# A six-layer linear-attention block with a quantised feed-forward: query and key products in three fp16 parts, softmax kept in PSUM, one merged root, a new instruction order

## What is computed

```python
mod = (_silu(c) @ wmod).reshape(8, 6, 1, -1)                     # sa, ca, ga, sb, cb, gb
ga = (2 * (ga >= 0) - 1) * jnp.maximum(jnp.abs(ga), 0.25)       # gb alike
h = _layernorm(x) * (1 + ca) + sa
for i in range(6):                                               # _L0_attn_ref
    xn = _layernorm(x, ln1_w[i], ln1_b[i])
    q, k, v = xn @ wq[i], xn @ wk[i], xn @ wv[i]                 # 8 heads of 16
    q = softmax(q, axis=-1); k = softmax(k, axis=-2)
    x = (q @ (k^T v)) @ wo[i] + bo[i] + x
    xn = _layernorm(x, ln2_w[i], ln2_b[i])
    x = leaky_relu(xn @ w1[i]) @ w2[i] + x                       # 128 -> 512 -> 128
x = x0 + ga * x
x = x + gb * fp4_ffn(_layernorm(x) * (1 + cb) + sb)              # 128 -> 352 -> 128
```

## Time and profile before

| | before |
|---|---|
| median of 3 runs | 1198.16 us |
| profiled execution, first to last instruction (span) | 1196.8 us |
| PE busy / DVE / ACT / POOL | 1129.7 / 1074.1 / 1035.2 / 1090.7 us |
| the chain that ended last | POOL 34%, PE 27%, issue 22%, DVE 10% |
| DMA | 190 MB, 159 GB/s |

### The profile page before, as it was taken

How to read it: one execution, slowest core, us unless ns; L and a number is a source line. 1 busy time by engine, 2 the same in 40 slices (tenths; PEclk the granted TensorE clock), 3 DMA queues, 4 the chain that set the end, 5 groups by cost and what they waited for, 6 DMA issues and landing times.

```text
span 1196.8 us, 28581 instructions
## 1 busy us (share of the span) xinstructions
PE 1129.7 (94%) x9722; PEld 864.8 (72%) x9722; DVE 1074.1 (90%) x2885; ACT 1035.2 (86%) x1776; POOL 1090.7 (91%) x920
## 2 busy tenths in 40 slices
PE   7787999999999999999999999999999888999996
PEld 5574687787777777777778778777777755565664
DVE  7889889999999999999999999999987479999973
ACT  5687999999999999999999999999998795767753
POOL 4888999999999999999999999999999888999762
PEclk8799999999999999999999999999999999999998
DMA  8121778768778777687777776866767420110000
GB/s 308 36 71 53 214 213 217 188 209 219 179 205 217 194 216 189 193 221 177 219 212 182 224 202 190 220 194 194 214 188 217 107 61 21 44 37 36 19 19 36
DMA packets 213857, 190.13 MB, mean 159 GB/s; under 512 B 113392, under 2 KB 192080, under 8 KB 213712
## 3 DMA queue, kind: packets, MB, share of 16 engines
q1 hardware_dynamic: 213712, 188.31, 56.3%
HBM read 87.06 MB, written 76.02 MB: 136 GB/s over the span
## 4 chain that ended last, share of the span: by engine, by line
POOL 34%; PE 27%; issue 22%; DVE 10%; ACT 3%; DMA 2%; SPq 2%; DVEq 0%; POOLq 0%; ACTq 0%
POOL hidden L1787 15%; POOL rows_split L1779 6%; POOL arena L1760 4%; POOL arena L1793 3%; PE pair_mlp L576 2%; PE pair_mlp L556 2%; PE ring_pair L615 2%; PE ring_pair L616 2%; PE ring_pair L617 2%; PE pair L567 2%; PE pair L599 2%; DVE ring_pair L1371 2%; DVE arena L1508 2%; PE pair_mlp L674 1%; DVE arena L1389 1%
## 5 line engine op out<-in xcount | busy, mean ns | idle before, releaser
L1787 POOL TENSOR_TENSOR hidden<-hidden 128x2048 f16<-128x2048 f32 x92 | 376.1, 4088 | 0.0
L883 ACT ACTIVATE hidden<-ring_pair,hidden_bias 128x512 f32<-128x512 f32 x384 | 245.6, 686 | 27.9 <-PE ring_pair L617 27.5
L892 ACT ACTIVATE hidden<-hidden 128x2048 f16<-128x2048 f32 x96 | 183.4, 1911 | 17.8 <-PE mlp L633 15.6
L1100 DVE BATCH_NORM_STATS2 bn<-x_all 128x6 f32<-128x128 f32 x896 | 184.2, 278 | 3.2 <-POOL x_all L1739 1.9
L1713 POOL TENSOR_TENSOR rstd<-ve,minus_half 128x8 f32<-128x8 f32 x104 | 170.5, 1640 | 0.0
L852 ACT ACTIVATE arena<-x_all,nmr,rstd 128x128 f32<-128x128 f32 x384 | 157.9, 495 | 0.0
L615 PE MATMUL ring_pair<-arena,halves 128*128 128x512 f16 x384 | 146.1, 381 | 4.5 <-DMA arena<-rows_split 2.8
L616 PE MATMUL ring_pair<-arena,halves 128*128 128x512 f16 x384 | 146.0, 380 | 0.0
L617 PE MATMUL ring_pair<-arena,halves 128*128 128x512 f16 x384 | 145.9, 380 | 0.0
L631 PE MATMUL mlp<-halves,hidden 128*128 128x128 f16 x768 | 135.9, 219 | 1.4 <-POOL hidden L1787 1.4
L633 PE MATMUL pair_mlp<-halves,hidden 128*128 128x128 f16 x768 | 136.5, 220 | 0.0
(11 more groups left out here) (206 smaller groups left out, 3145.1 us busy)
## 6 DMA issues: line engine op xcount, KB each, us to landing
n_away<-all_blocks SPq DMA_DIRECT2D x47, 512.0 KB, 3.3
norm_raw<-n_away SPq DMA_DIRECT2D x188, 128.0 KB, 3.0
k_away<-all_blocks SPq DMA_DIRECT2D x45, 512.0 KB, 2.8
q_away<-all_blocks SPq DMA_DIRECT2D x45, 512.0 KB, 3.3
arena<-k_away SPq DMA_DIRECT2D x180, 128.0 KB, 3.6
arena<-q_away SPq DMA_DIRECT2D x180, 128.0 KB, 3.6
x_all<-in_L_attn_x SPq DMA_DIRECT2D x8, 512.0 KB, 5.4
x_in<-in_L_attn_x SPq DMA_DIRECT2D x8, 512.0 KB, 4.0
```

The costliest lines, as they stand in the source:

```text
L883: act.activation(hidden_t[:, c * W + h * HALF:c * W + (h + 1) * HALF], ring[n % 2], ACT.Prelu, bias=hidden_bias[:, b:b + 1], scale=HIDDEN_ ...
L892: act.activation(half_rows(hidden_hi, h), half_rows(hidden_t, h), ACT.Copy).then_inc(hidden_hi_ready, 1)
L1100: last = nc.vector.bn_stats(bn[:, 6 * t:6 * t + 6], src(t))
L1787: pool.tensor_tensor(half_rows(hidden_lo, h), half_rows(hidden_t, h), half_rows(hidden_hi, h), ALU.subtract).then_inc(hidden_lo_ready, 1)
```

## The change

It has seven parts.

1. `product_k` and `product_q` use three fp16 products (rows high x weights high, rows high x weights low, rows low x weights high). The layer scale and the mean's subtraction are folded into `wq` and `wk` at the start (`fold_rows` on POOL, `fold_products` on PE), which are then scaled by powers of two (`bound_products`, `prepare_qk_downs`, `prepare_qk_scales` on DVE) and split (`qk_high` on ACT, `qk_low` on DVE). All six layers are prepared before the first key product. ACT `first_norm_high` takes the place of `first_norm_t`, POOL gets `first_norm_low`, DVE gets `scale_k`.
2. `shift_q` and `exp_q` work in place in S0, `sum_q` reads S0, and `normalise_q` moves from POOL to DVE. S0 is free only after it.
3. One root per iteration for both norms: ACT `root_guess` (Ln, then Exp), then Newton steps of POOL on 16 columns. `root1` and `root2` go.
4. `normalise1`: six tiles on POOL, two on ACT (three and five before).
5. The gates are computed on 8 rows at the start (6 steps) and spread by a matmul; `prepare_gates` goes.
6. The low parts of w1 and w2, and 8 of the 17 `round_weights` steps, move from DVE to POOL.
7. A new order on every engine; `keep_warm` and the direct path of item 0 (`turn_first_n`) go; the pipeline is one iteration deeper (`max_k(v - 3)`, `add_mlp(v - 8)`, `ITEMS + 16` iterations, feed-forward units woven in from v = 49 to 63).

```diff
-    GATE_STEPS = 18
+    GATE_STEPS = 6
-    POOL_TILES = 3
-    FIRST_N, FIRST = 1, 3
+    POOL_TILES = 6
+    FIRST_N, FIRST = 0, 3
...
+            def load_products():
+                for to, wt in ((wq_raw, wq), (wk_raw, wk)):
+                    sp.dma_start(to.rearrange("p (l o) -> p l o", l=DEPTH), wt.rearrange("l f o -> f l o")).then_inc(qk_loaded, 16)
...
+            def fold_products():
+                pe.wait_ge(qk_loaded, 2 * 16)
+                pe.wait_ge(fold_rows_ready, DEPTH)
+                for bank, raw in ((S0, wq_raw), (S1, wk_raw)):
+                    for l in range(DEPTH):
+                        last = nc.tensor.matmul(tile(bank, l), tile(fold_rows, l), tile(raw, l), start=True, stop=True)
+                    last.then_inc(qk_steps, 1)
...
             def product_k(i):
-                pe.wait_ge(norm1_t_ready, i + 1)
+                pe.wait_ge(norm1_hi_ready, i + 1)
+                pe.wait_ge(norm1_lo_ready, i + 1)
+                if i == 0:
+                    pe.wait_ge(qk_ready, DEPTH)
...
+                    nc.tensor.matmul(o, hi, rows_hi, start=True, stop=False)
+                    nc.tensor.matmul(o, lo, rows_hi, start=False, stop=False)
+                    last = nc.tensor.matmul(o, hi, rows_lo, start=False, stop=True)
...
             def product_q(i):
                 after(pe, x_mid_ready, i - 1)
+                after(pe, q_prob_ready, i)
                 for t in range(T):
-                    last = nc.tensor.matmul(tile(S0, t), tile(norm1_t, t), w, start=True, stop=True)
+                    nc.tensor.matmul(tile(S0, t), tile(norm1_hi, t), hi, start=True, stop=False)
+                    nc.tensor.matmul(tile(S0, t), tile(norm1_hi, t), lo, start=False, stop=False)
+                    last = nc.tensor.matmul(tile(S0, t), tile(norm1_lo, t), hi, start=False, stop=True)
...
             def exp_q(i):
-                act.activation(q_exp, q_exp, ACT.Exp).then_inc(q_exp_ready, 1)
+                act.activation(S0[:, :], S0[:, :], ACT.Exp, scale=qk_ups[:, i // B:i // B + 1]).then_inc(q_exp_ready, 1)
...
+            def root_guess(v):
+                act.activation(root_log[:, :], mv[:, :, 1], ACT.Ln, bias=eps_cols[:, 0:1]).then_inc(root_log_ready, 1)
+                act.activation(root_y[:, :], root_log[:, :], ACT.Exp, scale=-0.5).then_inc(root_y_ready, 1)
...
+            def scale_k(i):
+                nc.vector.tensor_scalar(k_neg_max, k_low, qk_ups[:, c:c + 1], None, ALU.mult).then_inc(k_max_ready, 1)
...
+            def normalise_q(i):
+                dve.wait_ge(q_rec_ready, i + 1)
+                after(dve, q_blocks_ready, i)
+                nc.vector.tensor_tensor(heads(q_prob), heads(S0[:, :]), q_rec[:, :].unsqueeze(2).to_broadcast((P, GROUPS, DH)),
+                                        ALU.mult).then_inc(q_prob_ready, 1)
...
+            def first_norm_low(i):
+                pool.wait_ge(norm1_hi_ready, i + 1)
+                after(pool, q_done, i)
+                pool.tensor_tensor(norm1_lo.rearrange("p (a m c) -> p a m c", a=2, c=32), norm1_raw.rearrange("p (m a c) -> p a m c", a=2, c=32),
+                                   norm1_hi.rearrange("p (a m c) -> p a m c", a=2, c=32), ALU.subtract).then_inc(norm1_lo_ready, 1)
```

955 lines of the change are left out of this document (531 added, 424 removed).

## The result

| | before | after |
|---|---|---|
| median of 4 runs each, side by side | 1198.1 us | 1240.4 us (1239.3 to 1242.2) |
| ratio | | 1.0348, 95% interval 1.0328 to 1.0368 |
| span of the profiled execution | 1196.8 us | 1237.5 us |
| PE / DVE / ACT / POOL busy | 1129.7 / 1074.1 / 1035.2 / 1090.7 | 1112.9 / 1107.8 / 1010.3 / 1056.1 |
| marker of item 0, of item 5 | 41.59, 145.19 | 68.75, 169.15 |

The changed kernel is 3.5% slower. The forecast was 1213 (1188 to 1228): the direction was right, the size outside the range. Of the 40.7 us between the two spans, **24.0 lie ahead of item 5's marker, 8.0 in the steady stage and 8.8 behind item 47's marker** (rounded). The forecast had 9.4, 3.0 and 2.2. The rest of the miss, 1.5 us, is that the median lies 2.9 us above the profiled span and not 1.4.

The account below looks back on a forecast made before the run. PE had no slack and POOL under half a microsecond per period; DVE would become busiest. Steady stage 3.0, start 9.4 and drain 2.2 add 14.6 to 1196.8, giving 1211.4; the median lies 1.4 higher, 1213 us, range 1188 to 1228.

Parts of the forecast that it names:

- The wait for `attend`: Steady stage, DVE between bias_context and add_attention: DVE stands still for 0.41 us per period.
- the clean period: Steady stage: DVE's work of 17.85 us plus a 0.4 us wait gives 18.25 us, between 18.1 and 18.6.
- The first rival: DVE, bias_context to add_attention: wait does not show, period 17.85, 17 us less; 1187 to 1195.7, chance 0.22.
- the surcharge: DVE passes moved to PSUM: two would cost 65 ns more each per item, +5.4 us, time 1218; not charged.
- The second loop: Rival: ring through ACT and POOL needs 0.5 us more, period 18.7, time 1232; chance 0.10.
- The cold PE: Rival: without fillers PE runs at 1.2 GHz for the first four items, +11 us, time 1224; chance 0.12.
- Start: Up to item 5's marker: DVE's work hardly changes, new waits add 9.4 us, from 0 to 20.
- two new waits: Start: centring begins later, +4.1 us; the first key product waits for all twelve split weight tiles, +5.3 us.
- the low bound: Start: 0 us added, as the new waits may sit in the 21 us of idle that existed before.
- Item 0's path through memory costs nothing: Start: item 0's rows are split at about 54 us, before the weights are ready at 58, so no charge.
- the weight steps: Steady stage: DVE's nine remaining steps add 7.4 us; POOL's eight add 3, from 0 to 8.
- the drain: From item 47's marker to the next unit's rows: 91 us instead of 89, +2.2, between -3 and +12.

Follow-up runs that it names:

- s2_neither: Changed kernel without the power-of-two search for wq and wk (scales 1) and without the eight gate products and their copies; 1231.4 us.
- d1_act_drain: Changed kernel with two steps of the first feed-forward unit, x_hat(0) and x_square(0), moved later on ACT in one drain iteration; 1243.3 us.
- e3: Changed kernel with five of DVE's weight steps moved behind the query normalisation; 1229.1 us.
- e4: Changed kernel with the first half of the MLP addition moved on DVE from ahead of bias_context to behind it (the cover); 1225.8 us.
- c4_start: Changed kernel with e3's and e4's edits, gate products moved into items 1 to 4, two last qk_high parts and w1's bounds reordered; 1215.8 us.

## Why the prediction was wrong

**What held.** DVE became the busiest engine's equal and sets the pace. The wait for `attend` that comes with the order is there in nearly every period (0.31 for 0.41), and the clean period is 18.26 for 18.25; that it fits so closely is luck, as the wait was 0.1 shorter and DVE's sum 0.1 longer than forecast. The first rival was right about the period, 17.89 for 17.85 with the wait covered, but not about its price: 17 us over the stage were expected, and the cover gave 9. The pieces were near as well: `normalise_q` 1.21 (1.14 to 1.22), `scale_k` 0.21 less its overlap (0.1 to 0.2), GpSimd's low parts of w1 1.19 (1.2), its weight steps 1.14 to 1.39 (1.4), the clean period's PE and POOL under it. Passes from PSUM cost nothing extra: `sum_q` has a mean of 1187 ns against 1206 from SBUF, so the surcharge that I weighed and left out is not there. The second loop did not show at 18.26. The cold PE came; in the items' first iterations it cost nothing that fillers gave back, but at the gates' products it lengthened the chain.

**The step that failed first: "Start".** I gave it +9.4, from 0 to 20; it is +24.0. The forecast's sum was: DVE's work up to item 5's marker "hardly changes", and two new waits cost 4.1 and 5.3. Both terms were too small. Up to that marker DVE is busy for 134.5 us (before 123.9) and idle for 34.7 (before 21.3): **+10.6 of work and +13.4 of waits.**

The work was put at nothing without a sum. By the rows' durations the twelve low parts of w1 and w2 took 15.3 us away; the five query normalisations brought 6.1, the low parts of wq and wk 4.1, the bounds and scales about 8, two more turns of the deeper pipeline 2.4, and smaller things the rest. About 4.9 us of the growth is the stretching beside GpSimd that is told below.

The waits came through a chain that I had too short: centring began at 18.6 (forecast 17.2), `qk_high` was done at 55.8 (49.0), the rows were split at 64.3 (54) and the weights ready at 64.5 (58). The eight gate products are one missing piece: the prediction names them nowhere, and on PE they stand for 12.3 us ahead of the fold. Without them item 0 comes 5.7 and item 5 7.8 us earlier.

The forecast also let the ramp win time back without saying so. With the weights at 58, item 0's marker would lie near 62 (4.1 us later, as measured), 20 us late, and yet item 5 was set near 155, 10 us late. Between the markers of items 0 and 5 lie 100.4 us now and 103.6 before, so only 3 are won back. The 21 us of DVE's idle time that the low bound leaned on were not slack: the new waits came on top of them. "Item 0's path through memory costs nothing" held (rows at 64.3, weights at 64.5), and s2_neither puts the path itself at only 2.6 us more than the direct one; but the queue ahead of that path, 10 us, was not seen.

**Second: the weight steps, "7.4" and "3".** Together 10.4 were forecast, the stage is 15.0 over 42 clean periods. Four of its periods held 12.1 us, since DVE's steps in them met a running GpSimd instruction; the other 38 share 2.9. I took 1.28 us from the earlier trace rows as the price of the instruction. It was the price at that place, beside the end of an instruction of GpSimd; in the middle of one it is up to 4.18, and free of it 0.5. The sum treated a step that is moved as if its duration moved with it. The same holds at the start: the 12-column `qk_ups` steps took 1.24 and 2.25 us beside GpSimd's two passes of 2.35, and the scaling of `bo_rows` 2.42 for 0.67.

**Third: the drain, +2.2.** Measured 7.8 to `x_rows(6)` and 1.0 behind it, within the bounds (-3 to +12) that I had set. The error that the traces show is in taking the idle time of before (12.8 us) over unchanged. It is 17.9, with PE waiting for ACT's hidden copies and for DVE behind the products of the first units; PE's own busy time is 2.7 longer, too. The only run on the drain (d1_act_drain) missed, so what causes these waits stays open.

Start, steps and drain were wrong in the same direction, each by an idle time, a duration or a sum of work that I had taken from the old order.

**Where the gain went.** PE's and POOL's saved time (17.5 and 46.5 us over the steady stage) became slack of these two. With e3 and e4 the steady stage is 762.0, 12 us better than before. The start and the drain, together +31 even in the best version (c4_start, 1215.8), eat it. None of the edits tried here makes the change pay. The fastest kernel of the study is the one before without its fillers, 1196.4, ratio 0.9975 (0.9961 to 0.9990).
